# Local masks by 64-row products on both halves of the array, adjacent spreading products, and a new local order

## The reference

```python
def attn_layer(x, Wqkv, qs, ksc, Wo):              # 16 heads of 64
    q, k, v = split(x @ Wqkv)
    q = l2norm(q) * qs;  k = l2norm(k) * ksc
    q = q * cos * scale + rotate_half(q) * sin * scale
    k = k * cos / scale + rotate_half(k) * sin / scale
    return local_attention(q, k, v) @ Wo
def local_attention(q, k, v):                      # windows of 32 positions
    # a query window sees its own window of keys and the one before it
    mask = (it < jb) | (it > jb + 32) | (jb == -1)
    sim = where(mask, -max, (bq @ bk2) * 8.0)
    return softmax(sim) @ bv2
def ffn_layer(x, g, bln, W1, b1, W2, b2):
    a, gate = split((layernorm(x) * g + bln) @ W1 + b1)
    return a * gelu(gate) @ W2 + b2
for i in range(6):
    x = attn_layer(shift_tokens(x), ...) + x
    x = ffn_layer(shift_tokens(x), ...) + x
```

## Time and profile before

| | us |
|---|---|
| median of 3 runs | 4000.34 |
| lowest, highest | 3998.91, 4010.74 |
| the profiled execution, whole | 3997.72 |
| its span, first to last instruction | 3995.8 |
| local stage, about | 740 to 3960 |
| PE busy | 3735.3 (93%) |
| DVE busy | 3008.7 (75%) |
| ACT busy | 2340.5 (59%) |
| POOL busy | 2315.1 (58%) |

### The profile page before, as it was taken

The page is one execution under the profiler, slowest core; times in us unless marked ns, Lnnn a source line. Parts: engine busy times, 40 slices in busy tenths (PEclk is TensorE's granted clock), DMA queues, the critical chain, the costliest instruction groups (busy, mean ns, idle before and its releaser), DMA issues.

```text
span 3995.8 us, 164202 instructions
## 1 busy us (share of the span) xinstructions
PE 3735.3 (93%) x73332; PEld 2172.9 (54%) x73332; DVE 3008.7 (75%) x3510; ACT 2340.5 (59%) x2850; POOL 2315.1 (58%) x1892
## 2 busy tenths in 40 slices
PE   7999999799998999999999999999899999999996
PEld 4655656455555555545555555555455555555553
DVE  7887888577777777767777777777777777777774
ACT  5565555455656565655555656565656565656653
POOL 4454555566665666655666656666556665666661
PEclk9999999899999999999999999999999999999998
DMA  1000000245443544444544434544354544454442
GB/s 58 5 5 7 5 4 23 59 107 118 100 100 91 121 98 115 103 94 97 116 104 110 98 93 111 120 96 107 85 120 98 118 97 97 107 116 99 105 105 81
DMA packets 162070, 349.09 MB, mean 87 GB/s; under 512 B 32606, under 2 KB 41948, under 8 KB 155100
## 3 DMA queue, kind: packets, MB, share of 16 engines
q1 hardware_dynamic: 161372, 338.58, 36.3%
HBM read 24.51 MB, written 4.19 MB: 7 GB/s over the span
## 4 chain that ended last, share of the span: by engine, by line
PE 77%; DVE 8%; issue 4%; DMA 4%; ACT 3%; SPq 2%; POOL 1%; ACTq 0%; DVEq 0%; POOLq 0%
PE psB L662 33%; PE psA L662 25%; PE psA L524 5%; PE psB L524 5%; DMA vev<-vo 3%; PE psA L714 3%; PE psB L740 2%; PE psB L714 2%; ACT pb L982 1%; DVE pt L1149 1%; PE psA L740 1%; SPq L471 1%; DVE top L1143 1%; SPq L487 1%; DMA kf<-h 1%
## 5 line engine op out<-in xcount | busy, mean ns | idle before, releaser
L1320 POOL TENSOR_TENSOR sq<-sq 128x512 f32<-128x512 f32 x384 | 490.1, 1295 | 483.3 <-ACT sq L952 483.1
L1315 POOL TENSOR_TENSOR h<-h,ts 128x512 f32<-128x512 f32 x384 | 490.3, 1277 | 210.9 <-DVE ts L1211 210.9
L1295 POOL TENSOR_TENSOR pt<-wk,pt 128x1024 f16<-128x1024 f32 (+3 forms) x256 | 371.5, 1472 | 342.7 <-DVE pt L1149 286.9
L1316 POOL TENSOR_TENSOR h<-h,ts 128x512 f32<-128x512 f32 x384 | 490.9, 1278 | 0.0
L952 ACT ACTIVATE sq<-psA 128x1024 f32<-128x1024 f32 x240 | 245.8, 1024 | 174.4 <-PE psA L662 169.8
L1203 DVE TENSOR_TENSOR h<-psA,t_rot 128x1024 f32<-128x1024 f32 x240 | 292.9, 1220 | 37.5 <-ACT sq L952 20.4
L662 PE MATMUL psB<-vev,ptb 64*32 64x65 f32 x9216 | 243.8, 225 | 56.4 <-ACT pb L982 37.1
L1211 DVE TENSOR_TENSOR ts<-psA,t_rot 128x1024 f32<-128x1024 f32 x240 | 291.2, 1213 | 3.1 <-POOL h L1316 3.1
L662 PEld LDWEIGHTS psB<-vev,ptb 64*32 64x32 f32 x9216 | 194.5, 106 | 173.3 <-issue 99.1
L1330 POOL TENSOR_SCALAR f_a<-f_a 128x512 f32<-128x512 f32 x48 | 31.2, 650 | 405.1 <-DVE f_a L1259 405.1
L1219 DVE TENSOR_TENSOR h<-h,psB 128x1024 f32<-128x1024 f32 x192 | 229.5, 1216 | 42.7 <-PE psB L662 40.7
(11 more groups left out here) (333 smaller groups left out, 10683.4 us busy)
## 6 DMA issues: line engine op xcount, KB each, us to landing
qf<-h SPq DMA_DIRECT2D x768, 136.0 KB
kf<-h SPq DMA_DIRECT2D x768, 136.0 KB
vev<-vo SPq DMA_DIRECT2D x192, 260.0 KB, 4.0
vev<-vo SPq DMA_DIRECT2D x192, 227.5 KB, 4.5
stage<-wqk SPq DMA_DIRECT2D x12, 512.0 KB, 4.6
stage<-wvl SPq DMA_DIRECT2D x12, 256.0 KB, 5.3
stage<-wof SPq DMA_DIRECT2D x6, 512.0 KB, 5.1
xb<-xt SPq DMA_DIRECT2D x8, 256.0 KB, 6.8
```

The costliest lines, as they stand in the source:

```text
L1295: e.tensor_tensor(pt[g][pr][:, :, 1, o:o + w], wk[(slot_of(s)[0] - 1) % SLOTS][:, :, 0:w], pt[g][pr][:, :, 0, o:o + w], ALU.subtract).then ...
L1315: e.tensor_tensor(halves_of(h, 0), halves_of(h, 0), t[1], ALU.subtract)
L1316: e.tensor_tensor(halves_of(h, 1), halves_of(h, 1), t[0], ALU.add).then_inc(ended["ad"])
L1320: e.tensor_tensor(sqb[c][:, 0, :], sqb[c][:, 0, :], sqb[c][:, 1, :], ALU.add).then_inc(ended["qa"])
```

## The change

1. The mask of a score tile was written by two products of 128 rows and 512 columns, one per bank: an identity as the stationary side, the mask (128 queries x 4 x 64) as the moving side. Now the mask itself is the stationary side, 64 keys (rows) by 128 queries, once for the first quarter of windows (whose first window has no predecessor) and once for the other three; a 64x64 identity is the moving side, repeated. A tile takes four products of 64 rows: 128 and 384 columns, each on both halves of the array. The constants are laid out for it: `t_masks` has 448 columns instead of 384.

2. All five orders of the local stage are new. In particular `bc10 bc11` and `bc00 bc01` now stand side by side in `TENSOR`.

```diff
-    lmask = np.where(ok, 0.0, NEG).reshape(128, NT * 2 * W)
+    lmask = np.where(ok, 0.0, NEG).reshape(128, NT, 2 * W)
+    lsel = [np.tile(lmask[:, t].T, (2, 1)) for t in range(2)]
...
-    masks = np.concatenate([np.eye(128), lmask] + parts, 1)
+    masks = np.concatenate([np.eye(128)] + lsel + [np.tile(np.eye(2 * W), (2, 1))] + parts, 1)
...
 TENSOR = (
-    "vp00:A ot00:B pj10:A pj11:B sc100:B tp01:A sc101 sc102 sc103 pj13:A pj12:A ng10 pv011:B pv010:B ss1:B "
+    "pv001:A pj12:B tp01:A ot00:A sc100:B sc101 sc102 sc103 la:A pj13:B pv010:A ng10 lb:A pv011:A ss1:B tp10:B "
+    "sc110:B sc111 sc112 sc113 ot01:B ng11 vp11:A f0:A pv100:B pv101:B bc10:B bc11:B tp11:A vp10:A pv111:A ot10:B "
+    "pj00:A+1 pv110:B pj01:A+1 pj03:B+1 f1:B f2:A sc000:A+1 sc001+1 sc002+1 sc003+1 pj02:B+1 ng00+1 ot11:A fo:B "
+    "ss0:B+1 sc010:A+1 sc011+1 vp00:B+1 pj11:A+1 sc012+1 sc013+1 tp00:B+1 vp01:B+1 ng01+1 pv000:B+1 bc00:B+1 "
+    "bc01:A+1 op:A pj10:B+1 "
...
 SYNC = (
-    "dm00+1 dm01+1 dm02+1 st0 st1 dm03+1 vd0+1 dm10+1 dm11+1 dm13+1 dm12+1 vd1+1 "
+    "dm01+1 dm02+1 vd0+1 dm11+1 dm10+1 st0+1 dm12+1 dm13+1 vd1+1 st1+1 dm00+2 dm03+2 "
...
-        t_masks = sb("t_masks", [128, 128 + NT * 2 * W], BF16)
+        t_masks = sb("t_masks", [128, 384 + 2 * W], BF16)
         identb = t_masks[:, 0:128]
-        lmask = t_masks[:, 128:].rearrange("p (t s) -> p t s", t=NT)
+        lsel = t_masks[:, 128:384].rearrange("p (t q) -> p t q", t=2)
+        keyid = t_masks[:, 384:384 + 2 * W]
...
-                        for x in range(2):
-                            mm(o[:, 512 * x:512 * x + 512].rearrange("p (t q s) -> p t q s", t=NT, q=2), identb,
-                               lmask.unsqueeze(2).to_broadcast([128, NT, 2, 2 * W]), True, False)
+                        for m, (at, n) in enumerate(((0, 2), (128, 6))):
+                            for x in range(2):
+                                rows, at_x = slice(64 * x, 64 * x + 64), 512 * x + at
+                                mm(o[:, at_x:at_x + 64 * n].rearrange("p (a s) -> p a s", a=n), lsel[rows, m, :],
+                                   keyid[rows, :].unsqueeze(1).to_broadcast([64, n, 2 * W]), m == 0, False,
+                                   tile_position=(64 * x, 0))
```

More of the change, by code:

```diff
@@ L139 @@
 TENSOR = (
[5 rows of a table removed]
[5 rows of a table added]
 )
 SCALAR = (
-    "ve11 oe10 sq00+1 sq02+1 ve01+1 sq03+1 oe11 nr0+1 ns0+1 ex00+1 lq+1 lw+1 tb1+1 te00+1 ex01+1 lr+1 oe00+1 "
-    "sq10+1 ve00+1 sq11+1 te01+1 sq13+1 sq12+1 ex10+1 xh+2 nr1+1 ns1+1 oe01+1 te10+1 oh ex11+1 ge1+1 wh0+1 ge2+1 "
-    "ge0+1 ve10+1 te11+1 sq01+2 wh1+1 "
+    "lw sq13 ex10 lr nr1 te10 ns1 ex11 oe01 ve11 ge0 te11 xh+1 ve10 wh1 oe10 sq00+1 sq01+1 sq03+1 ge2 ge1 sq02+1 "
+    "ex00+1 oe11 nr0+1 ns0+1 ve00+1 tb1+1 sq11+1 te00+1 ve01+1 ex01+1 sq10+1 sq12+1 oh te01+1 oe00+1 wh0+1 lq+1 "
 )
 VECTOR = (
[3 rows of a table removed]
[4 rows of a table added]
 )
 GPSIMD = (
-    "lx qa10 ad10 qa11 qa13 qa12 ad11 xl+1 ad13 nw1 ad12 qa01+1 ad01+1 ad00+1 qa00+1 qa03+1 qa02+1 ad03+1 nw0+1 "
-    "ad02+1 "
+    "nw0 ad02 qa11 ad11 qa10 ad10 qa12 qa13 lx nw1 ad12 ad13 xl+1 qa00+1 qa01+1 ad00+1 ad01+1 qa03+1 ad03+1 "
+    "qa02+1 "
 )
 SYNC = (
-    "dm00+1 dm01+1 dm02+1 st0 st1 dm03+1 vd0+1 dm10+1 dm11+1 dm13+1 dm12+1 vd1+1 "
+    "dm01+1 dm02+1 vd0+1 dm11+1 dm10+1 st0+1 dm12+1 dm13+1 vd1+1 st1+1 dm00+2 dm03+2 "
 )
@@ L278, in program @@
         wbig = flat(ot[0])[:, 0:3 * 1024]
-        st_masks, st_left, t_wmod = (flat(ot[1])[:, a:z] for a, z in ((0, 1152), (1152, 1408), (1408, 2176)))
+        st_masks, st_left, t_wmod = (flat(ot[1])[:, a:z] for a, z in ((0, 1216), (1216, 1472), (1472, 2240)))
         acc = [w[3] for w in wu]
@@ L1111, in vector @@
                             e.wait_ge(s_const, 48)
-                            e.tensor_copy(t_masks[:, :], st_masks[:, 0:384])
-                            e.tensor_copy(t_half.rearrange("p h m n -> p (h m n)"), st_masks[:, 384:1152])
+                            e.tensor_copy(t_masks[:, :], st_masks[:, 0:448])
+                            e.tensor_copy(t_half.rearrange("p h m n -> p (h m n)"), st_masks[:, 448:1216])
                             e.tensor_copy(flat(t_sel), st_left[:, :]).then_inc(s_masks)
```

## The result

The changed kernel takes **4017.57 us** (median of 11 runs, 4007.35 to 4025.83), the kernel before, beside it on the same chip, 4001.82 us (3995.18 to 4011.95). The ratio is 1.004, with an interval of 1.003 to 1.0049: slower by 0.4%, where the prediction said 3950 and faster. The profiled span grew from 3995.8 to 4009.7 us.

What follows compares the result with a forecast made beforehand. PE was taken as the bound, working for all but 1.2 us of an image. The terms -40 - 35 - 37 + 12 - 5 + 19 + 24 + 14 = -48 gave 3950 us (own range 3915 to 3985).

Steps and rivals of the forecast that it cites:

- masks: Ahead of the scores, the new mask products save 0.21 us on each of 4 tiles per image: -40 us.
- wait of `pv010`: PE's wait for the exponential ahead of `pv010`, once per image, goes as `pv010` moves to ring A: -37 us.
- changes of mode: Tiling mode changes in one turn of `TENSOR` fall from 44 to 38, at 0.12 us each: -35 us.
- `pv101`, `bc10`, `bc11`: Behind `pv101`, `bc10` waits 0.25 us for DVE's `nm100`; `bc11` starts where `bc10` ends, without overlap: +12 us.
- `bc00`, `bc01`: `bc01` needs exponential `ex01`, starts 0.8 us behind `bc00` and overlaps it by 0.1 us: -5 us (0 to -45).
- `ng11`: Only `ot01` stands between the tile's last score and `ng11`, so PE waits for DVE's maximum: +19 us.
- `sc100`: `sc100` waits for the transfers of chunks 0 and 1, 0.5 us per image: +24 us (0 to +53).
- `ng00`, `fo`, `ss0`: Three places on PE with no distance to spare, taken at 0.3 us per image: +14 us (0 to +100).
- Whatever is taken off PE is worth its full length unless a new wait takes it back.: Premise for PE's work in an image: removed work shortens the run fully, except for new waits; no separate size.
- All other takes of a tile have more than 1.5 us of distance.: Beyond the listed waits, PE steps taking over a tile have over 1.5 us to the step before; nothing added.
- rival "slower": POOL's string of `qa` and `ad` ahead of `ss0` runs late, paid once per image: 4012 us; chance 0.13.
- rival that the four products overlap: Both pairs of spreading products, `bc10 bc11` and `bc00 bc01`, overlap on the array: about 3854 us; chance 0.1.

Runs made afterwards that it cites:

- scores_together: Kernel before with `tp01` moved ahead of `sc100`, `tp10` ahead of `sc110`, `ot01` behind `sc113` (four score steps in a row): 4081.09 us, ratio 1.0213.
- bc_later: Changed kernel with `bc10 bc11` moved behind `vp10` instead of right behind `pv101`: 4111.92 us, ratio 1.0261.

## Why the prediction was wrong

Its numbers against measured ones, each a difference of step costs per image, times 48:

| term | forecast | measured |
|---|---|---|
| masks | -40 | -38 (4 x 0.20) |
| wait of `pv010` | -37 | -39 (`pv011` 1.65 to 0.84) |
| changes of mode | -35 | about -37 (what is left of the steps' minima) |
| `pv101`, `bc10`, `bc11` | +12 | +16 (2.98 to 3.32) |
| `bc00`, `bc01` | -5 | -12 (2.16 to 1.91) |
| `ng11` | +19 | +23 (`ot01` 1.02 to 1.50) |
| `sc100` | +24 | +30 (`ot00` 0.93 to 1.55) |
| `ng00`, `fo`, `ss0` | +14 | about -3 (by PE's waits, 13.0 us before, 10.9 after, in 41 images) |
| sum | -48 | about -60 |

The minima are the shortest cost of each step: their sum falls by 1.71 us, of which the terms above explain all but 0.77. That row is a remainder and was not isolated.

- *"Whatever is taken off PE is worth its full length unless a new wait takes it back."* This step failed. There is a third taker, which is no wait for a tile. Border idle grew from 32.4 to 60.7 us between 1000 and 3700, 0.7 per image, **+33** in 48. It was in the trace before, in the 60.7 us of "issue" (about 39 of them are border idle), and I had read no row of it: 0.8 us per image that belonged in the question what a denser order does. scores_together shows the cause. A fourth follows from it, the clock: in the 46 images between the first `fo` and the 47th, the trace has ten stretches at a granted clock of 0.50 before and nineteen after. PE works in them for 41.2 and 78.2 us. At half speed the difference costs about **+18** (an estimate, half of 37). Ahead of each of the nineteen PE had stood 1.7 to 2.9 us; thirteen of these pauses are at a border, against two of the ten before.
- *"PE works for all but 1.2 us of an image."* In the trace before PE is idle 2.9 us per image over these 46 images (0.8 of it at borders, part of the rest at the ends of layers). A record runs for 63.3 us per image, not for the 64.1 of the unit costs.
- *"All other takes of a tile have more than 1.5 us of distance."* False for four takes. `tp10` waits for `ts13` (6.9 us in 36 times by idle time, **+8** by the cost of `ss1`, 1.04 to 1.21). `ot11` takes the tile of `f2`, and in 36 of 41 images it starts 0.05 us behind the DVE instruction that reads it last; `ng00` ahead of it costs 0.65 us in most images instead of 0.43 (**+9**). PE's products show no idle time there, because the record of `ng00` lasts beyond it (1236.01 to 1236.60 in the image below). `pj02` starts 0.05 to 0.06 us behind `ts` in 27 of 41 images (`sc003` ahead of it went from 0.39 to 0.72, border idle included). `sc100` waits for `ts10` in 27 images, as said; this is part of its +30. The take of `ot11` (timelines of DVE and PE, after):

```profile
1235.70 0.74 DVE L1275 SCALAR_TENSOR_TENSOR f_g<-psA,b1s,f_g 85x512 f32<-85x512 f32 x1
...
1236.50 1.09 PE L748 MATMUL psA<-t_mats,ob 128*128 128x128 f32 x8
```

- *`ng00`, `fo`, `ss0` at +14.* Not found: the three places together cost about as much as before. `fo` had waited 2.6 us at the end of each layer (13.0 us in all) and no longer does; `ng00` now waits 1.6 us there (8.3), and `ss0` 0.1 in half of the images (2.6). POOL's string `sq` is named for 10.1 us in 13 times after and 9.1 in 3 before. So the rival "slower" named its mechanism wrongly, though slower came true. (The 14.8 us that PE was said to have up to `ss0` add up to 14.6.)
- *The start and the end were put at nothing, or not counted.* A new order has a new filling and a new emptying. At the start `fo` of the first image is 8.0 us late; border idle up to there is 9.2 us, before it was 3.5. At the end `f1` and `f2` of the last image but one stand behind `pv` steps that wait, and PE pauses for longer, so its clock falls. The windows of the last stretch, after and then before (the number ahead of the last two is the granted clock):

```profile
3940.00:4009.00 69.00, 34.84 (x204) 14.89 (x204) 24.75 (x34) 10.73 (x14) 3.10 (x3) 0.71 0.09 33
```

```profile
3940.00:3995.00 55.00, 25.43 (x262) 12.03 (x239) 24.98 (x35) 11.24 (x14) 3.10 (x3) 0.78 0.11 39
```

  and the last `fo`, after and then before:

```profile
3988.78 4.51 PE L667 MATMUL psB<-f_g,w2r 128*128 128x512 f32 x6 [2.26 <-issue]
```

```profile
3976.53 2.82 PE L662 MATMUL psB<-f_g,w2r 128*128 128x512 f32 x6 [1.61 <-DVE f_g L1267]
```

  Six records take 4.51 us instead of 2.82. Start and end together: **+15**.

One sum closes, because it only divides PE's time. Between the `fo` of the first and of the 47th image:

| us | before | after | difference |
|---|---|---|---|
| idle at borders | 35.4 | 69.1 | +33.7 |
| idle ahead of steps (waits) | 95.9 | 102.9 | +7.0 |
| a record runs | 2913.0 | 2871.1 | -41.9 |
| whole | 3044.35 | 3043.11 | -1.2 |

The forecast for the same 46 images was -77 of work (masks, changes of mode, overlap of `bc00` and `bc01`) and +31 of waits. The work that was taken off is 41.9 us, and about 60 if the 18 that the lower clock added are left out (an estimate). Idle time is counted here from the end of the last record, so that the draining in front of each wait counts as work; this is why the waits look smaller than in the table of step costs, and the work saved too. What of the missing 17 us is such draining and what is a cheaper change of mode than the forecast's 0.12 us was not separated. By step costs it is -60 (the table) + 33 (borders) + 18 (clock) + 8 (`tp10`) + 9 (`ot11`) = +8 where 1.2 us less was measured. These costs overlap (`sc003`, `ot00` and `ot01` hold border idle too), and gains that I had not counted (`lb` 0.23 less, its wait for the transfers into `vev`; `ng01` 0.18) and the take of `pj02` are not in it. So the direction of each term is read from the trace, and their sizes to about 10 us.

What was right: the masks' 0.31 us (0.32), the wait for `nm100` ahead of `bc10` and the four products one after the other (1.96 us, forecast 2.0), both read from the earlier trace rows; the wait of `ng11`, and that of `sc100` for the transfers in 21 images; no wait of PE that names the table loads. The forecast of `bc00` and `bc01` had the mechanism (`bc01` starts 0.05 us behind the exponential in 40 of 40 images) and was low in size, -5 for -12. The rival that the four products overlap is true of the array (1.14 us in bc_later) and false of this order. The rule cited with it (the Trainium skill, "TensorE: Matmul & The Clock Gate", section Packing small matmuls) is met in kind: 1.14 instead of 1.96.

## What to carry to other kernels

Taking work off the busiest engine gives its length only if instructions come fast enough and it does not stand so long that its clock falls: count records per us, not only busy time, and leave a long step between steps of many short products. When an order changes, its filling and emptying are terms of the sum, and every wait ahead of a step has a distance to be written down, not only the ones that look tight. A step that stands behind another which frees its input late is best moved by one place, with the longest step that waits for nothing put between: that was worth 0.6% here.

## What the runs showed of the hardware

PE's instructions come in blocks of 256 records, and PE stood ahead of about every eighth border (63 of 508) in the changed kernel, up to 3.6 us in the middle of a step. The Trainium skill, "Runtime: NRT & Kernel Launch", section Instruction fetch mechanics, says that the instruction memory is refilled in blocks of 16 KiB, 256 instructions, and that crossing a border is mostly hidden because instructions are issued more slowly than they are filled in. The traces agree with the block (16,384-byte packets, each idle time at the same place of 256), and disagree with the second part for runs of short products: 256 records within 1.8 us outran the supply, and it cost 1% before and 2% after (39.5 and 78.7 us of 4000).

A pause at a border costs its length and then, at times, the clock. Behind the 2.06 us of the timeline above, the products of 512 columns stand 0.42 us apart (1475.05 to 1475.47) where they otherwise stand 0.22 apart. The windows of three stretches (the pause, what follows, and later in the image; granted clock third from the end) say the same:

```profile
1471.00:1473.00 2.00, 0.00 (x0) 0.00 (x0) 1.53 (x2) 0.00 (x0) 1.94 (x2) 1.00 0.03 4
1474.60:1477.00 2.40, 2.40 (x7) 0.76 (x5) 0.00 (x0) 1.08 (x2) 0.00 (x0) 0.50 0.00 0
1482.00:1484.00 2.00, 2.00 (x113) 1.61 (x114) 1.19 (x3) 1.59 (x3) 1.53 (x2) 1.00 0.93 176
```

A granted clock of 0.50 is the lower of PE's two levels, 1.2 GHz. It follows a pause of only 2 us in full work, and doubles the time of what runs in it. Over the whole profiled execution the mean granted clock is 0.981 before and 0.975 after. Not every such pause is followed by it: behind the longest one, 3.64 us at 2216 us, the clock stayed at 1.00.
